# Differential attention with a gated feed-forward: queries and keys stored whole and split per head by DVE

## The reference

```python
q1, q2, k1, k2, v = (heads(x @ W) for W in (Wq1, Wq2, Wk1, Wk2, Wv))
a1 = softmax(causal(q1 @ k1.T / 4)); a2 = softmax(causal(q2 @ k2.T / 4))
out = (a1 - lam * a2) @ v                       # lam: one number per head
x = layernorm(x + (layernorm(out) * (1 - LAM_INIT)) @ Wo)
h = silu(x @ w1.T * s1) * (x @ w2.T * s2)
h = gelu(h @ h1.T * hs1); h = gelu(h @ h2.T * hs2)
x = layernorm(x + (h @ w3.T) * s3)
```

## Time and profile before

| | us |
|---|---|
| median of 3 runs | 2055.02 (2047.17 to 2059.04) |
| the profiled execution, its own time | 2058.76 |
| its span, first to last instruction | 2057.0 |
| PE busy | 1917.9 |
| ACT busy | 1468.7 |
| DVE busy | 724.0 |

### The profile page before, as it was taken

One profiled execution on the slowest core, in us unless ns is written; L12 is line 12 of the kernel. 1 busy time (PEld: TensorE's weight loads), 2 busy tenths in 40 slices (PEclk: granted clock), 3 DMA queues, 4 the chain that ended last, 5 costly groups with the idle time before them and its releaser, 6 DMA issues. The chain is left out here.

```text
span 2057.0 us, 32689 instructions
## 1 busy us (share of the span) xinstructions
PE 1917.9 (93%) x12400; PEld 1091.7 (53%) x12400; DVE 724.0 (35%) x1543; ACT 1468.7 (71%) x1876; POOL 200.3 (10%) x300
## 2 busy tenths in 40 slices
PE   7995499999999999999999997599999999999996
PEld 6883133333333333333333332488888788888885
DVE  5776012222122221222112221445463545445342
ACT  5663499999999999999999997244454445445452
POOL 0001011111111111111111110000000000000000
PEclk9997699999999999999999999699999999999998
DMA  8997906643466434653356510200000000000000
GB/s 265 364 348 216 140 2 84 84 58 53 59 84 84 54 54 62 84 73 54 47 78 84 72 24 11 72 22 11 32 11 31 22 31 31 12 31 11 11 11 12
DMA packets 137048, 148.55 MB, mean 72 GB/s; under 512 B 76000, under 2 KB 108256, under 8 KB 133760
## 3 DMA queue, kind: packets, MB, share of 16 engines
q1 hardware_dynamic: 134768, 140.55, 34.2%
q10 hardware_dynamic: 1888, 5.24, 1.3%
q0 software_dynamic: 240, 0.66, 0.2%
HBM read 90.85 MB, written 55.57 MB: 71 GB/s over the span
## 5 line engine op out<-in xcount | busy, mean ns | idle before, releaser
L808 ACT ACTIVATE attn_probs<-attn_s_ps 128x1024 f32<-128x1024 f32 (+2 forms) x1152 | 1014.0, 1042 | 75.3 <-PE attn_s_ps L827 71.5
L847 PE MATMUL attn_sums_ps<-attn_probs,heads_v 128*32 128x512 f32 (+3 forms) x5120 | 603.1, 543 | 0.6 <-issue 0.6
L827 PE MATMUL attn_s_ps<-heads_q,heads_k 50*128 50x512 f32 (+3 forms) x2560 | 472.5, 431 | 67.2 <-DMA heads_q<-shift 49.5
L827 PEld LDWEIGHTS attn_s_ps<-heads_q,heads_k 50*128 50x128 f32 x2560 | 216.6, 185 | 543.1 <-ACT attn_probs L808 457.9
L1331 ACT ACTIVATE split_whole<-split_hid_ps,hs 128x512 f32<-128x512 f32 x128 | 88.3, 690 | 274.4 <-PE split_hid_ps L1245 274.2
L892 DVE COPY attn_sums_sb<-attn_sums_ps 128x512 f32<-128x512 f32 x64 | 44.3, 692 | 639.1 <-PE attn_sums_ps L847 635.7
L792 POOL TENSOR_SCALAR_AFFINE_SELECT attn_probs<-attn_probs 128x512 f32<-128x512 f32 x256 | 160.4, 635 | 919.8 <-ACT attn_probs L808 917.9
L1245 PE MATMUL split_hid_ps<-split_hid_b,h2t_r 128*128 128x512 f32 x1024 | 240.6, 392 | 0.0
L1245 PE MATMUL split_hid_ps<-split_hid_a,h1t_r 128*128 128x512 f32 x1024 | 238.0, 391 | 0.0
L1245 PEld LDWEIGHTS split_hid_ps<-split_hid_a,h1t_r 128*128 128x128 f32 x1024 | 190.0, 188 | 41.1 <-DVE split_hid_a L1473 1.3
L1245 PEld LDWEIGHTS split_hid_ps<-split_hid_b,h2t_r 128*128 128x128 f32 x1024 | 189.8, 188 | 38.0
(11 more groups left out here) (123 smaller groups left out, 1571.2 us busy)
## 6 DMA issues: line engine op xcount, KB each, us to landing
qk_parts<-proj_parts SPq DMA_DIRECT2D x64, 512.0 KB, 5.7
heads_q<-qk_parts SPq DMA_DIRECT2D x90, 256.0 KB
heads_k<-qk_parts SPq DMA_DIRECT2D x90, 256.0 KB
proj_w_rows<-in_L_ffn_h_w SPq DMA_DIRECT2D x16, 512.0 KB, 6.8
values<-proj_v SPq DMA_DIRECT2D x8, 1024.0 KB, 6.0
diffs<-attn_diff SPq DMA_DIRECT2D x32, 256.0 KB, 4.5
split_heads<-diffs SPq DMA_DIRECT2D x8, 1024.0 KB, 5.7
heads_v<-values SPq DMA_DIRECT2D x15, 512.0 KB
```

The lines of the kernel that those rows point to most:

```text
L808: nc.scalar.activation(weights, side_by_side, ACT.Exp, scale=SCALE).then_inc(exp_done, 1)
L827: last = nc.tensor.matmul(s_ps[n % SLOTS][:, s, place * width:(place + 1) * width], k_sb[u][rows, b * SEQ + j * PARTS:b * SEQ + (j + 1) * ...
L847: last = nc.tensor.matmul(sums[c * D:(c + 1) * D, off:TILE], v_sb[u][:, b * KEY_BLOCKS + j, :], probs[k % PROBS][:, b, s, off:TILE], start ...
```

## The change

- The host turns `x` and the feed-forward weights and lays every input out so that each partition reads one long piece. The transposes of both, on PE, with their copies, are gone.
- ACT copies queries and keys out of PSUM whole; SP stores them once, in `qk_raw`. The buffers are still four.
- Head 0's stacks, its values, the ones and the shift table are written during projection; the shift of head 0 is added by DVE in its place (`add_shift`) at the start of attention.
- For each later head the raw rows are loaded three times into the stack, ones are loaded from a small DRAM tensor `ones` into the rows behind them, then the shift rows, and DVE turns this in place into the stack of high and low parts (`cut_piece`: a rounded copy into `spare`, then `high * low_rows + raw`, in pieces of 1024 columns, eight per head). The raw and the rounded stack are the same memory (`twins`).
- The values get a semaphore of their own and are loaded last.
- Semaphores of the later stages get their first values from POOL during projection; the credit blocks are gone. The scales' loads and the small vectors go from SP and POOL to ACT's queue.
- In the attention's tile two multiplications by the reciprocals become one.

```diff
-    qk_parts = nc.dram_tensor("qk_parts", (2, PARTS_KEPT, EMBED, 2, TOKENS), F32, kind="Internal").ap()
+    qk_raw = nc.dram_tensor("qk_raw", (2, EMBED, 2, TOKENS), F32, kind="Internal").ap()
+    ones = nc.dram_tensor("ones", (HALF_ROWS - SCORE_ROWS, TOKENS), F32, kind="Internal").ap()
...
+    def twins(self, name, shape):
+
+        with self.nc.sbuf_tensor(f"{self.phase}_{name}_raw", shape, F32) as raw:
+            pass
+        return raw, self.sb(name, shape, F32R)
...
-def give_credits(nc, credits):
-    with nc.Block() as block:
-        @block.sync
-        def _(sp):
-            for sem, n in credits:
-                sp.sem_inc(sem, n)
+def give_credits(eng, credits):
+    for sem, n in credits:
+        eng.sem_inc(sem, n)
...
@@ project_phase, sync @@
+            sp.wait_ge(preset_set, 2)
+            for a in range(SHIFT_ROWS):
+                sp.dma_start(shift[a].rearrange("h s n -> (h s n)").rearrange("(p n) -> p n", p=PARTS),
+                             v_sb[a][:, 0:HEADS // 2, :, :].rearrange("p h s d -> p (h s d)")).then_inc(preset_stored, 16)
...
+                    sp.wait_ge(qk_copied, n + 1)
+                    sp.dma_start(qk_raw[kind // 2, c * PARTS:(c + 1) * PARTS, kind % 2, bass.ts(t, TILE)], copies[n % COPIES][:, :]).then_inc(copy_stored[n % COPIES], 16)
+                    if c == 0:
+                        if n == 0:
+                            sp.wait_ge(rows_set, 4)
+                            sp.dma_start(ones, k0[SCORE_ROWS:HALF_ROWS, :]).then_inc(ones_stored, 16)
+                        stack, places = ((q0, QUERY_PLACES), (k0, KEY_PLACES))[kind // 2]
+                        for place in range(len(places)):
+                            row = (kind % 2) * HALF_ROWS + place * HEAD_DIM
+                            sp.dma_start(stack[row:row + HEAD_DIM, bass.ts(t, TILE)], copies[n % COPIES][0:HEAD_DIM, :]).then_inc(copy_stored[n % COPIES], 16)
...
@@ project_phase, scalar @@
+            act.dma_start(keep["s3"][:, :], s3.partition_broadcast(PARTS)).then_inc(scales_loaded, 16)
+                for name, s in (("s1", s1), ("s2", s2), ("hs1", hs1), ("hs2", hs2)):
+                    act.dma_start(keep[name][:, :], s.rearrange("(c p) -> p c", p=PARTS)).then_inc(scales_loaded, 16)
+            high_x(0)
...
@@ project_phase, tensor @@
-                    if m in GROUP_AT:
-                        for j in range(k):
-                            last = nc.tensor.transpose(w_ps[:, j, :], w_rows[u][:, col + j * PARTS:col + (j + 1) * PARTS], ident[:, :])
-                    if more and m == X_AT:
-                        turn_x(t + 1, 1 - u, r + u)
...
+def cut_piece(nc, dve, raw, stack, high, low_rows, made_high, i, made):
+
+    nc.vector.tensor_copy(high, raw).then_inc(made_high, 1)
+    dve.wait_ge(made_high, i + 1)
+    nc.vector.scalar_tensor_tensor(stack, high.bitcast(F32), low_rows, raw, ALU.mult, ALU.add).then_inc(made, 1)
+    dve.wait_ge(made, i + 1)
...
+def load_stacks(dma, q, k, qk_raw, ones, sem, head, query_ones):
     for which, stack, places in ((0, q, QUERY_PLACES), (1, k, KEY_PLACES)):
         for s in range(2):
+            for n in range(len(places)):
                 row = s * HALF_ROWS + n * HEAD_DIM
+                dma(stack[row:row + HEAD_DIM, :], qk_raw[which, bass.ts(head, HEAD_DIM), s, :]).then_inc(sem, 16)
+            row = s * HALF_ROWS + (query_ones, SCORE_ROWS)[which]
+            dma(stack[row:(s + 1) * HALF_ROWS, :], ones[0:(s + 1) * HALF_ROWS - row, :]).then_inc(sem, 16)
...
@@ attention_phase, sync @@
                     sp.wait_ge(probs_free, PROBS + NS * h)
-                    load_head(sp.dma_start, heads, qk_parts, values, h + 1, 1 - u)
-                    load_shift(sp.dma_start, heads, shift, h + 1, 1 - u)
+                    load_stacks(sp.dma_start, q_raw[1 - u], k_raw[1 - u], qk_raw, ones, stacks_loaded[1 - u], h + 1, STACK_ROWS)
+                    load_shift(sp.dma_start, q_raw[1 - u], shift, stacks_loaded[1 - u], h + 1, slice(0, TOKENS))
+                    sp.dma_start(v_sb[1 - u][:, :, :], values[h + 1]).then_inc(values_loaded[1 - u], 16)
...
@@ attention_phase, tensor @@
-                if n == 0:
-                    pe.wait_ge(loaded[u], 16 * HEAD_LOADS * r + 16 * HEAD_LOADS)
+                if first and STEPS[k][1] == 0 and batches[0] == 0:
+                    pe.wait_ge(shift_added, 2 * (t + 1))
+                    if t == QUERY_TILES - 1:
+                        pe.wait_ge(cut_done, TAIL)
+                if n == 0 and not first:
+                    pe.wait_ge(values_loaded[u], 16 * ((h + 1) // 2))
+                    pe.wait_ge(cut_done, TAIL + CUTS * h)
...
@@ attention_phase, vector @@
+            def add_shift(t):
+                for s in range(2):
+                    rows = slice(s * HALF_ROWS + ONES_ROW, (s + 1) * HALF_ROWS)
+                    both = q_sb[0][rows, :].rearrange("p (b n) -> p b n", b=BATCH)[:, :, bass.ts(t, TILE)]
+                    nc.vector.tensor_scalar(both, both.bitcast(F32), keep["shift_add"][rows, 0:1], None, ALU.add).then_inc(shift_added, 1)
+            def cut_stacks(h, u, first, last):
+                if first == 0:
+                    dve.wait_ge(stacks_loaded[u], 16 * HEAD_DMAS * ((h + 1) // 2))
+                for i in range(first, last):
+                    name, piece = CUT_ORDER[i]
+                    low_rows = keep["query_rows"][:, 0:1] if name == "q" else keep["low_rows"][:, 1:2]
+                    cut_piece(nc, dve, heads[f"{name}_raw"][u][:, bass.ts(piece, PIECE)], heads[name][u][:, bass.ts(piece, PIECE)], spare[:, :], low_rows, cut_high, TAIL + CUTS * (h - 1) + i, cut_done)
...
-                nc.vector.tensor_tensor(first[:, :, :], raw[:, :, 0, 0:D - 1], recip[:, :, 0:1].to_broadcast(wide), ALU.mult).then_inc(vec, 1)
-                nc.vector.tensor_tensor(second[:, :, :], raw[:, :, 1, 0:D - 1], recip[:, :, 1:2].to_broadcast(wide), ALU.mult).then_inc(vec, 1)
+                nc.vector.tensor_tensor(sums[:, :, 0:D - 1], sums[:, :, 0:D - 1],
+                                        recip[:, :, :].rearrange("p k s -> p (k s)").unsqueeze(2).to_broadcast([PARTS, 2 * SUBS * BATCH, D - 1]), ALU.mult).then_inc(vec, 1)
...
             for h in range(HEADS):
-                for t in range(QUERY_TILES):
-                    tile(h, t)
+                tile(h, 0)
+                tile(h, 1)
+                if h < LAST:
+                    cut_stacks(h + 1, 1 - h % 2, 0, EARLY_CUTS)
+                tile(h, 2)
+                if h < LAST:
+                    cut_stacks(h + 1, 1 - h % 2, EARLY_CUTS, CUTS)
+                tile(h, 3)
```

More of the change, by code:

```diff
@@ L96, in layer_kernel @@
+                more_head_buffers(room, heads)
+                maximum_phase(nc, keep, max_sems, heads, qk_raw, shift, ones)
+                attention_phase(nc, keep, attn_sems, heads, qk_raw, shift, ones, values, diffs)
             finish_phase(nc, keep, sems, "split", True, rounded, x, wo, diffs, out)
-        whole_w = {name: sb(f"{name}_f", shape) for name, shape in FFN_SHAPES}
-        turn_weights_phase(nc, keep, ffn_w, whole_w)
-        finish_phase(nc, keep, sems, "full", False, whole_w, x, wo, diffs, out)
+        whole_w = sb("ffn_f", [PARTS, CHUNKS, CHUNK])
@@ L417, in _ @@
[L417 to L425 removed]
+                    dve.wait_ge(qk_copied, n + 1)
@@ L991, in finish_sems @@
-def finish_sems(nc, room):
+                for k in range(CHUNKS):
+                    sp.dma_start(whole[:, k, :], ffn[k]).then_inc(loaded, 16)
+                sp.wait_ge(loaded, 16 * CHUNKS)
+def finish_sems(room):
     wo_loaded = room.sem("wo_loaded")
```

724 lines of the change are left out of this document (345 added, 379 removed).

## The result

The changed kernel takes 2272.3 us (median of 4 runs, 2267.4 to 2273.4); the kernel before takes 2055.9 us (4 runs, 2047.2 to 2059.0). The ratio is 1.1056, with a 95% interval of 1.1037 to 1.1076: 10.6% slower. The profiled execution took 2271.9 us, with a span of 2268.9 us and a mean granted clock of 0.926.

The account below looks back on a forecast made before the run. ACT was taken to bound attention and PE, with transfers close behind, projection. From 2058.8 us, 54 off for the front, 2 off for the finish and 200 added for 14 stalled heads gave 2203, said as 2200; range 2085 to 2285.

Parts of the forecast that it names:

- the rival in which more is lost: Heads 1 to 14 lose 19.7 us each, or projection bound by transfers, 20 us later: around 2275 us; chance 0.16.
- The chain: In heads 1 to 14, DVE's wait and four cuts delay sums copy, PE's transposes, scores, ACT: 14.3 us a head.
- The second wait: At a head's end: the four late cuts, ending at +71, would be late next if the first stall were gone.
- The issue at +11.6: SP starts the next head's loads 11.6 us after a head's first exponential, behind the previous head's differences' store.
- The ones: Attention: four new loads of ones per head, 60 rows of 16 KB, take 8.1 us at 121 GB/s.
- The start: Start of projection: scales on ACT's queue take 12 us, first matmul at 20.5 us (bounds 16 and 24).
- The tile: Projection: PE needs 16.9 us per tile, transfers 16 us; 18 us taken, bounds 17.4 and 20.
- the change doesn't shorten projection: Rival: PE waits for SP's 25 issues or four copy buffers; 20 us per tile, total up 16 to 20 us.
- The landing: Attention: the next head's stacks land 50.0 us after a head's first exponential; bounds +44 and +53.
- The finish: Feed-forward: one credit block less ahead of it and less empty code behind the last store, 2 us gained.
- The price of a stop: Heads 1 to 14: PE 14.2 us late, minus 1.9 for its lead, plus 2.0 for half clock: 14.3 us.
- loads that land early: Rival: stacks land by +37.7, so PE's lead covers the stall; total 2000 us; chance 0.10.

Follow-up runs that it names:

- Experiments 1 to 3: Changed kernel with all cuts behind query tile 2 (2157.0 us), then DVE's wait there too (2123.5), then PE also waiting only for pieces it reads (2027.3).
- Experiment 2: Changed kernel with all eight cuts and DVE's wait for the stacks moved behind query tile 2: 2123.5 us, ratio 1.0339.
- Experiment 5: Changed kernel loading only 4 of 60 rows of ones per head, cuts in two halves, two early cuts instead of four: 2356.7 us, ratio 1.1467.
- experiments 1 to 5: Five edits against the changed kernel, same projection: Experiments 1 to 3; next head's loads issued before the last quarter of differences is stored (2118.4 us); Experiment 5.
- Experiment 3: Changed kernel with cuts and DVE's wait behind query tile 2, PE waiting only for pieces it reads: 2027.3 us, ratio 0.9880.
- experiment 8: Experiment 3 plus scales' loads and projection's values' store on POOL's queue: 2006.2 us, ratio 0.9780; on another chip 2013.3 us, ratio 0.9785.

## Why the prediction was right, and where its sizes were off

The forecast was 2200 us in a range of 2085 to 2285; measured were 2272.3. The direction and the mechanism hold, and the time lies at the range's upper end, close to the rival in which more is lost (2275), whose price per head (19.7 us) is also nearer to the 18.0 measured than the forecast's 14.3. That this rival's total fits so well is luck: it had a dearer stop or a projection 20 us later, and what came was most of the one (3.7 us of its 5.4 per head) together with most of the other (16 us).

**What held.**
- *The chain.* DVE in order, the stacks' landing, four cuts, the sums' copy, the transposes, the scores, ACT. Experiments 1 to 3 take it apart link by link: without the cuts ahead of tile 2 a head is 73.7 us, with the wait gone too 72.0, and with PE's waits made finer 64.6.
- *The second wait.* The prediction said that the late cuts would be late once the first stall is gone. Experiment 2 shows it.
- *The ends.* Heads 0 and 15 are not lengthened (68.6 and 64.4 us, as before).
- *The count.* Heads 1 to 14; DVE's 15 waits for the stacks are those and one of 2.3 us in head 0, which stops nobody.
- *The cuts.* Four in 8.19 us, forecast 8.2.
- *The issue at +11.6*, behind the differences' store, exact.
- *The ones.* 8.1 us for 60 rows was forecast at 121 GB/s. Experiment 5 gives 6.9 us for 56 rows, 7.4 for 60 in proportion. The Trainium skill, "DMA: Bandwidth & Descriptors", Specifications, gives some 27 GiB/s per engine, and by it the prediction's estimate for the ones was 2.3 us. Sixteen engines at that rate make it 2.1. The measurement disagrees for loads into so few partitions, and it decides.

**What was off, by the terms of the sum.**

| term | forecast | measured |
|---|---|---|
| first matmul | 20.5 | 25.7 |
| tile of projection | 18 | 19.4 |
| first scores, gain | 54 | 38.0 |
| stacks land | +50.0 | +52.3 |
| sums copied back, late by | 14.2 | 17.0 |
| a head, longer by | 14.3 | 18.0, head 5 too |
| 14 heads | 200 | 251.4 |
| finish | -2 | -1.4 |

- *The start.* I took 12 us for the scales on ACT's queue, between bounds of 8 and 15.2. They took 15.4, as on SP's queue before, so the second figure needed no bound. The load of ACT's table behind them, 1.28 us, wasn't in my sum.
- *The tile.* I took PE's 16.9 us as the base and added little, because transfers of 16 us lay beside it. They don't lie beside it freely. Four copy buffers tie them together: ACT can't copy until a store issued four groups before has landed, and it waited 44.3 us for that. I also took 10 us per tile for SP's 25 issues; in the trace SP is issuing, or held up in an issue, for some 14.5 of the 19.4 us. Which of the two makes the stores late isn't shown. My own rival "the change doesn't shorten projection" named both; it deserved to be the forecast. The gain of the front also differs between traces of the same projection: first scores come between 188.2 and 195.5 us in the kernel after and experiments 1 to 5, a gain of 37 to 44 us.
- *The landing.* 2.3 us later than forecast. The ones explain none of it (they cost less than I took), so the other loads, with the values issued behind them, took longer than the 29.4 us that I read from the earlier trace rows. What among them did isn't settled.
- *The finish.* It won 1.8 us between the last exponential and the feed-forward stage's first matmul and 1.5 behind the last store's issue, the two places that the forecast named, and lost 1.9 in between, for which I have no cause.
- *The price of a stop.* Of the 3.7 us between 14.3 and head 5's 18.0, 2.3 are the landing and 0.45 the transposes, which ran at half clock (1.11 us instead of 0.66). The other 0.9 are lead and clock together. I took -1.9 and +2.0, and they came to +1.0. ACT stopped at +45.5, just when the sums used to come back (+45.4), so PE's lead over ACT hid next to nothing. The clock was back some 4 us after PE went on, where I had taken 10 us from the earlier trace rows.

By these terms, with the -0.1 us of head 0: -38.0 - 0.1 + 251.4 - 1.4 = +211.9, which is the difference of the spans.

**Without the stall, the change is a gain.** The prediction had this only for loads that land early (2000 us). Experiment 3 has it with loads as late as in the kernel after: it keeps all the new work and is 1.2% faster than before. In the version of experiment 8 DVE is busy 280.5 us of the 600 from 600 to 1200 us, instead of 130.3, and a head takes 65.1 us on average against 64.9. The loss came from where the cuts stood, not from what they are.

## What to carry to other kernels

Before work is put between two steps of an engine that works in order, ask who waits for the later step and when the new work's input arrives: here a load due at +62 was made due at +41, and the engine that paid was not the one that waited. When a stall is moved, look for the next waiter, and let each consumer wait only for the piece that it reads; 96 of the 245 us of this repair came from PE's wait. And where nearly full resources are coupled by a few buffers, as here PE, the transfers and SP's queue, don't take the largest of them as the time of the whole.

## What the runs showed that I had not expected

- Issuing four small vectors of scales from ACT's queue took 15.4 us and held back the first matmul until 25.7 us; from POOL's queue the four took 3.6 us.
- A store issued on SP's queue right behind a 1 MB store of values took up to 5.74 us to issue instead of 0.43. With the values on another queue the longest took 2.6 us, but SP's queue stood waiting for other engines for less of the time, not more (8.4 us of 100 instead of 24.9).
- A vector operation on 50 partitions took as long as on 128: 0.69 and 1.28 us for 1024 columns.
- Traces of the same projection code put the start of its last matmul between 174.9 and 182.4 us.
